# Expert layers of a macaron block: routing in one piece with gathered tiles, or by batches with rows scattered to regions

## The reference, cut to what matters

```python
x = x + 0.5 * ffn(layernorm(x), ...)
x = x + attn(layernorm(x), ...)          # 16 heads of 8, rotary, causal
x = x + 0.5 * ffn(layernorm(x), ...)

def ffn(x, Wr, br, ln_g, ln_b, W1, b1, W2, b2):   # 8 experts, one for each token
    p = softmax(xt @ Wr + br)
    gates, idx = max(p), argmax(p)
    xn = layernorm(xt) * ln_g + ln_b               # 128 features
    h = relu(xn @ W1[idx] + b1[idx])               # 512 wide
    y = (h @ W2[idx] + b2[idx]) * gates
```

## Time and profile before

| | us |
|---|---|
| median of three runs | 973.03 |
| the profiled execution | 971.15 |
| its span, first to last instruction | 969.2 |
| busy: TensorE / VectorE / ScalarE / GpSimd | 781.0 / 658.9 / 530.0 / 354.1 |
| first expert layer, until its last write-back is issued | 0 to 180 |
| attention with its projections | 188 to 793 |
| output projection | 794 to 810 |
| second expert layer | 810 to 969 |

### The profile page before, as it was taken

One profiled execution on the slowest core, in us unless ns is written; L12 is line 12 of the kernel. 1 busy time (PEld: TensorE's weight loads), 2 busy tenths in 40 slices (PEclk: granted clock), 3 DMA queues, 4 the chain that ended last, 5 costly groups with the idle time before them and its releaser, 6 DMA issues. The chain is left out here.

```text
span 969.2 us, 17210 instructions
## 1 busy us (share of the span) xinstructions
PE 781.0 (81%) x5494; PEld 426.3 (44%) x5494; DVE 658.9 (68%) x1821; ACT 530.0 (55%) x1126; POOL 354.1 (37%) x635
## 2 busy tenths in 40 slices
PE   2839777258459999999999999999999988578874
PEld 2838777234212333333333333333333337567773
DVE  4475565279867787787877878778787209656563
ACT  1206666215404667766677666766667643146663
POOL 5006777217812222332223322233222210047774
PEclk9659999769856999999999999999999779589998
DMA  9062222214572022210222102221020000532221
GB/s 323 34 174 71 76 74 72 64 36 116 155 189 35 2 50 52 50 44 10 50 51 51 43 10 50 51 50 43 10 51 3 1 1 1 146 81 73 78 77 24
DMA packets 42083, 62.32 MB, mean 64 GB/s; under 512 B 7843, under 2 KB 33453, under 8 KB 40592
## 3 DMA queue, kind: packets, MB, share of 16 engines
q1 hardware_dynamic: 33248, 45.76, 18.7%
q0 software_dynamic: 6240, 14.48, 5.6%
q10 hardware_dynamic: 2512, 1.06, 0.4%
HBM read 39.87 MB, written 21.92 MB: 64 GB/s over the span
## 5 line engine op out<-in xcount | busy, mean ns | idle before, releaser
L1235 DVE CUSTOM_DVE_ANT_0 cst<-psS,cst 128x768 bf16<-128x768 f32 (+7 forms) x512 | 364.4, 755 | 103.0 <-PE psS L1109 100.7
L1199 ACT ACTIVATE prob<-psST 128x512 f32<-128x512 f32 (+3 forms) x768 | 323.8, 495 | 143.3 <-PE psST L1134 139.8
L1148 PE MATMUL a_psO<-prob,vs 128*32 128x512 f32 (+3 forms) x1536 | 168.5, 511 | 0.9 <-POOL prob L1320 0.7
L1319 POOL TENSOR_TENSOR a_gate<-a_zeros 1x1 f32<-1x1 f32 x128 | 23.6, 184 | 335.1 <-ACT prob L1199 335.1
L1134 PE MATMUL psST<-a_qs,ks 75*128 75x512 bf16 (+1 forms) x480 | 123.9, 327 | 5.7 <-ACT prob L1199 3.3
L654 POOL DMA_INDIRECT g_row<-rows,f_there_number x78 | 77.8, 998 | 133.3 <-SPq L500 110.1
L1109 PE MATMUL psS<-ks,a_qs 72*128 72x512 bf16 (+2 forms) x480 | 116.6, 332 | 5.3 <-DVE a_rowmax L1235 5.2
L1109 PE MATMUL psS<-ks,qs 72*128 72x512 bf16 (+3 forms) x288 | 76.6, 359 | 24.5 <-DMA qs<-q_split 17.1
L555 PE MATMUL g_psH<-g_xnT,g_w1s 128*128 128x128 f32 x624 | 83.6, 277 | 2.4 <-ACT g_xnT L583 2.4
L1134 PE MATMUL psST<-qs,ks 75*128 75x512 bf16 (+3 forms) x288 | 80.3, 351 | 6.3 <-ACT prob L1199 5.1
L565 PE MATMUL g_psY<-g_w2s,g_hidT 128*128 128x128 f32 x624 | 83.4, 277 | 1.1 <-ACT g_hidT L590 1.1
(11 more groups left out here) (154 smaller groups left out, 923.0 us busy)
## 6 DMA issues: line engine op xcount, KB each, us to landing
ks<-k_split SPq DMA_DIRECT2D x48, 192.0 KB
rows<-tok SPq DMA_DIRECT2D x8, 1028.0 KB, 11.1
a_qs<-q_split SPq DMA_DIRECT2D x60, 96.0 KB
k_split<-p_part SPq DMA_DIRECT2D x40, 128.0 KB, 2.3
qs<-q_split SPq DMA_DIRECT2D x36, 96.0 KB
q_split<-p_part SPq DMA_DIRECT2D x24, 128.0 KB, 2.3
w<-in_Wb SPq DMA_DIRECT2D x1, 2064.0 KB, 10.7
w<-in_W SPq DMA_DIRECT2D x1, 2048.0 KB, 15.8
```

Source lines behind the costliest of these rows:

```text
L1148: last = nc.tensor.matmul(psO[32 * h:32 * h + 32, c0:c0 + w], vs[r][:, j, h, :], prob[:, u % RING, h, 0:w], start=(j == 0), stop=(u + 1 in ...
L1199: nc.scalar.activation(prob[:, u % RING, h, 0:w], psST[(u * QH + h) % 3][:, 0:w], ACT.Exp, scale=SCALE).then_inc(exp_done, 1)
L1235: last = nc.vector.tensor_tensor_reduce(out=out[:, a * CH:a * CH + width], in0=ps[:, a * CH:a * CH + width], in1=mask_row[:, S - width:], ...
```

## The change

The output projection moves into the second layer's block. Routing goes by four batches of 1024 tokens (TB = 8 columns). TensorE's order is a list: project (second layer), router, ranks. VectorE does `statistics(b)` and `choose(b)`; the reciprocal roots are made without ScalarE, by a shifted integer as a first value and three Newton steps, for both norms at once. ScalarE normalises four of a batch's eight columns, VectorE the others. A token's place is known once its batch is ranked: each expert has its own region of 4224 rows in DRAM, `base` carries on how far each is filled, and GpSimd scatters the batch's eight columns there by 128 rows of 1032 bytes (the token's number is now the last column). The slot and tile matrices, their 64 products, the store of `tok` and the gathers go. `tables` computes each tile's expert and first row. SP writes 128 rows of padding behind each region, waits for the scatters, and loads the tiles as blocks of consecutive rows, up to eight ahead; GpSimd keeps the write-back alone, its indices read from the row itself. Everything of a layer is one block. The weights are loaded only after x has arrived, and the warm-up before the tile loop is 28 x 4 products, queued behind `ranks(3)`. Not shown below: `choose` is the selection of before on 64 columns a batch; ScalarE follows TensorE's list (normalisations and copies for a router, copies for a project, the exponential for ranks); the tile loop's code for TensorE, ScalarE and VectorE is as before; `tables` is 17 small steps.

```diff
-TW = 2 * D + 1
-HALF_GATE = 2 * D
+TW = 2 * D + 2
+HALF_GATE, TOKEN = 2 * D, 2 * D + 1
...
-WARM = (18, 16)
+WARM = (18, 28)
+SCATTERS, YR = 4, 4
...
+REGION = B * S + P
+PADS = E * REGION
...
 def load_weights(sp, n):
 
+    for b in range(B):
+        sp.wait_ge(n.x_loaded[b], 16)
...
+        order = []
+        if r == 1:
+            order += [("project", 0), ("project", 1)]
+        order += [("router", 0), ("router", 1)]
+        for b in range(B):
+            if r == 1 and b + 2 < B:
+                order.append(("project", b + 2))
+            order.append(("ranks", b))
+            if b + 2 < B:
+                order.append(("router", b + 2))
...
+            def statistics(b):
+                sl = slice(b * TB, (b + 1) * TB)
+                if r == 0:
+                    dve.wait_ge(n.x_loaded[b], 16)
+                for g in range(b * PB, (b + 1) * PB):
+                    if r == 1:
+                        dve.wait_ge(projected, g + 1)
+                        x = n.tok[:, g * CB:(g + 1) * CB, 0:D]
+                        nc.vector.tensor_tensor(x, x, out_ps[g % 2][:, :].rearrange("p (j d) -> p j d", j=CB),
+                                                ALU.add).then_inc(added, 1)
+                        dve.wait_ge(added, g + 1)
+                    for t in range(g * CB, (g + 1) * CB):
+                        link.then(nc.vector.bn_stats(n.stats[:, t, :], n.tok[:, t, 0:D]))
+                link.join()
+                mean, var = n.mean[:, sl], n.var[:, sl]
+                even, odd, sq_even, sq_odd = (n.stats[:, sl, k] for k in (1, 4, 2, 5))
+                link(nc.vector.tensor_tensor(mean, even, odd, ALU.add))
+                link(nc.vector.tensor_scalar(mean, mean, 0.5, None, ALU.mult))
+                link(nc.vector.tensor_tensor(var, sq_even, sq_odd, ALU.add))
+                link(nc.vector.tensor_tensor(even, even, odd, ALU.subtract))
+                link(nc.vector.scalar_tensor_tensor(even, even, 0.25, even, ALU.mult, ALU.mult))
+                link(nc.vector.scalar_tensor_tensor(var, var, 1.0 / D, even, ALU.mult, ALU.add))
+                sh, ro, co = shift[:, b, :, :], root[:, b, :, :], corr[:, b, :, :]
+                link(nc.vector.tensor_scalar(shift[:, b, 0, :], var, EPS, None, ALU.add))
+                link(nc.vector.tensor_scalar(shift[:, b, 1, :], var, 1.0 + EPS, EPS * EPS, ALU.mult, ALU.add))
+                link(nc.vector.tensor_scalar(ro.bitcast(I32), sh.bitcast(I32), 1, None, ALU.logical_shift_right))
+                link(nc.vector.tensor_scalar(ro.bitcast(I32), ro.bitcast(I32), -1.0, FIRST_ROOT, ALU.mult, ALU.add))
+                for _ in range(3):
+                    link(nc.vector.scalar_tensor_tensor(co, ro, -0.5, ro, ALU.mult, ALU.mult))
+                    link(nc.vector.tensor_tensor(co, co, sh, ALU.mult))
+                    link(nc.vector.scalar_tensor_tensor(ro, co, 1.5, ro, ALU.add, ALU.mult))
+                nc.vector.scalar_tensor_tensor(offset[:, sl], mean, -1.0, root[:, b, 1, :],
+                                               ALU.mult, ALU.mult).then_inc(scales_ready, 1)
+                for t in range(b * TB + 1, (b + 1) * TB, 2):
                     nc.vector.tensor_scalar(n.shared[:, t, :], n.tok[:, t, 0:D], n.mean[:, t:t + 1],
+                                            root[:, b, 1, t % TB:t % TB + 1],
+                                            ALU.subtract, ALU.mult).then_inc(odd_normed, 1)
+                link(nc.vector.tensor_tensor(inv_u[:, sl], shift[:, b, 1, :], root[:, b, 1, :], ALU.mult))
+                link(nc.vector.tensor_tensor(inv_u[:, sl], inv_u[:, sl], root[:, b, 0, :], ALU.mult))
...
+                dve.wait_ge(ranks_done, b + 1)
+                link(nc.vector.tensor_tensor(rk, part(b, 1), base[:, b, :].unsqueeze(1).to_broadcast([P, TB, E]),
+                                             ALU.add))
+                dve.wait_ge(onehot_ready, b + 1)
+                link(nc.vector.tensor_tensor(rk, rk, onehot[:, sl, :], ALU.mult))
+                link(nc.vector.reduce_sum(pk, rk, AX.X))
+                nc.vector.tensor_copy(place[:, sl], pk).then_inc(placed, 1)
+                link(nc.vector.tensor_tensor(base[:, b + 1, :], base[:, b, :], part(b, 2)[:, 0, :], ALU.add))
...
+            statistics(0)
+            statistics(1)
+            choose(0)
+            for b in range(2, B):
+                statistics(b)
+                choose(b - 1)
+            choose(B - 1)
+            tables()
+            dve.wait_ge(tiles_known, 2)
...
+            def project(g, u):
+                pe.wait_ge(turned_copied, u + 1)
+                wait(pe, added, g - 1)
+                for j in range(CB):
+                    last = nc.tensor.matmul(out_ps[g % 2][:, j * P:(j + 1) * P], xT[u % 2][:, j * P:(j + 1) * P],
+                                            n.wproj[:, 5, :], start=True, stop=True)
+                last.then_inc(multiplied, 1)
+                pe.wait_ge(multiplied, u + 1)
+                pe.sem_inc(projected, 1)
...
+            warm_up(nc, pe, n, psW, WARM[1])
...
+            rows = n.rows_dram[r]
+            sp.wait_ge(pool_chain, 2)
+            sp.dma_start(rows[PADS:PADS + P, :], pad[:, :]).then_inc(pads_stored, 16)
+            sp.wait_ge(counted, 1)
+            for e in range(E):
+                at = sp.value_load(pad_row[0:1, e:e + 1], min_val=e * REGION, max_val=e * REGION + B * S)
+                sp.dma_start(rows[ds(at, P), :], pad[:, :]).then_inc(pads_stored, 16)
+            sp.wait_ge(pads_stored, 16 * (E + 1))
+            for k in range(SCATTERS):
+                sp.wait_ge(scattered[k], 16 * NT // SCATTERS)
+            sp.wait_ge(tiles_known, 2)
+            for t in range(NS):
+                k = t % LR
+                at = sp.value_load(tile_row[0:1, t:t + 1], min_val=0, max_val=PADS)
+                wait(sp, y_stored[t % YR], 16 * ((t - LR) // YR + 1))
+                sp.dma_start(row[k][:, :], rows[ds(at, P), :]).then_inc(loaded[k], 16)
...
+            sent = 0
+            for b in range(B):
+                pool.wait_ge(gates_ready, b + 1)
+                pool.wait_ge(placed, b + 1)
+                for t in range(b * TB, (b + 1) * TB):
+                    wait(pool, scattered[sent % SCATTERS], 16 * (sent // SCATTERS))
+                    pool.indirect_dma_start(
+                        out=n.rows_dram[r][:, :],
+                        out_offset=bass.IndirectOffsetOnAxis(ap=place[:, t:t + 1], axis=0),
+                        in_=n.tok[:, t, :], in_offset=None).then_inc(scattered[sent % SCATTERS], 16)
+                    sent += 1
```

More of the change, by code:

```diff
@@ L271, in ffn @@
 def ffn(nc, n, r, target):
[L277 to L279 removed]
+    G = NT // CB
+    PB = TB // CB
+    with ExitStack() as ctx:
         def sb(name, shape, dt=F32):
[L281 to L370 removed]
@@ L417, in _ @@
[L417 to L427 removed]
+                link(nc.vector.tensor_tensor(last[:, :], first[:, :], ntile[:, :], ALU.add))
```

685 lines of the change are left out of this document (299 added, 386 removed).

## The result

The changed kernel takes **980.35 us** in the median of 20 runs (971.72 to 983.23), the kernel before 966.58 (20 runs, 962.56 to 975.91): a ratio of 1.0119, 95% interval 1.0095 to 1.0144. The forecast was 970 with most of its weight on faster or no change; it is slower, by 1.2%. The forecast also started from a median of three runs, 973.03, that lies 6.45 above the median of twenty. The profiled execution of the changed kernel took 981.57 us, its span is 979.6. To see what belongs to the change I also use a second pair of traces, from another chip: spans of 964.3 before and 970.4 after.

What follows compares the result with a forecast made beforehand. GpSimd's write-back and gather issues were taken to bound the tile loop. -39.3 + 4.8 + (1.1 to 5.9) + (23.4 to 33.0) = -10.0 to +4.4, taken -2.8: 968.4, about 970 us against the median; range 952 to 992.

Steps and rivals of the forecast that it cites:

- the middle: Whole kernel: the value taken within the sum's -10.0 to +4.4 us, -2.8, from routing clocks of 0.56 and 0.84.
- 38 steps, two layers: Tile loop without gathers: 2.03 us a step, 77.1 a layer in place of 97.2 and 96.3, so -39.3 us.
- first transpose, layer one: Layer one's routing in four batches: first transpose at 76.7 to 81.5 us instead of 75.61, +1.1 to +5.9.
- first projection addition to first transpose, layer two: Layer two's routing with projection: first transpose at 881.0 to 890.6 us instead of 857.59, +23.4 to +33.0.
- restart at half clock: Tile loop's start: warm-up ends 12 us early, first tiles run at 1.2 GHz, 2.4 us lost a layer, +4.8.
- the cold end: Routing with TensorE at the low clock throughout: the upper ends of its terms, +4.4 us for the whole sum.
- twenty small steps at 0.205: Routing, VectorE's statistics of each batch: mean, variance, shift trick and Newton rounds take 4.1 us.
- four of eight normalisations at 0.26: Routing, VectorE's statistics of each batch: its share of the normalisations takes 1.0 us, the other four go to ScalarE.
- The attention is not touched: Attention, 203 to 793 us, most of the span: left out of the forecast's sum as unchanged.
- the rival of slow scatters: Routing: GpSimd's scatters slower than its gathers; at 2.0 us each, 11 us a layer, 992 in all; chance 0.13.
- a loop near 2.6: Tile loop: SP's load or a row buffer's return comes late, step stays near 2.6 us, about 1009; chance 0.07.
- everything at its good end: Routing keeps 2.4 GHz (10.0 us gained), tiles run at 1.92 (8.4 more): about 955; chance 0.32.

Runs made afterwards that it cites:

- e_weights: The changed kernel with the weights loaded only after the first batch's gates are known: 991.69 us, 0.963 of the kernel before on its chip.
- e_dummy: The changed kernel with four kinds of VectorE operations run once on scratch ahead of layer one's first batch: 996.19 us, 0.964 of the kernel before.
- a_att: The changed kernel with unused TensorE products filling two idle stretches at the attention's start: 992.24 us, 0.963 of the kernel before on its chip.
- b_att: The kernel before with unused TensorE products filling two idle stretches at the attention's start: 1041.66 us, 1.006 of the unedited kernel before on its chip.
- e_poolloads: The changed kernel with block loads issued by GpSimd, one behind every write-back, in place of SP: 1038.19 us (one run).
- e_hoist: The changed kernel with VectorE's read of the expert number put ahead of the weigh addition: 977.01 us, 0.945 of the kernel before on its chip.
- e_twice3: The changed kernel with the last batch's eight scatters sent twice in each layer: 1003.28 us (one run).
- e_order: The changed kernel with layer two's projections one place earlier in TensorE's and ScalarE's order: 983.16 us, 0.954 of a kernel before of 1032.5.

## Why the prediction was wrong

From the profile of before (span 969.2) to that of after (979.6), beside the middle that I took:

| term | forecast | measured |
|---|---|---|
| 38 steps, two layers | -39.3 | -16.5 and -15.1 = -31.6 |
| first transpose, layer one | +1.1 to +5.9, taken +3.5 | 87.51 - 75.61 = +11.9 |
| first projection addition to first transpose, layer two | +23.4 to +33.0, taken +28.2 | 91.6 - 59.9 = +31.7 |
| restart at half clock | +4.8 | from transpose to first bias addition, 3.2 for 2.07, twice = +2.3; the rest is in the steps |
| attention | 0 | -2.6 |
| all else | 0 | -1.3 |
| sum | -10.0 to +4.4, taken -2.8 | +10.4 |

The two sums are 13.2 us apart. Layer one's first transpose makes 8.4 of it, 2.4 by the middle and 6.0 beyond even the cold end; the steps and the restart make 5.2; layer two's first transpose makes 3.5, all of it by the middle; the attention and all else take 3.9 off. So more than one step failed: the middle cost 5.9, and with the cold end, +4.4, the sum would still have been 6 us short.

**The first step that failed is "so I take the middle, -2.8".** I had put the sum's cold end at +4.4 and argued for a mixture from 0.56 and 0.84 of before's clock. The same section said that routing is now spread thinner. The traces show 0.50 from 20 to 64 us and 0.50 to 0.57 over most of layer two's routing, and waits at, and 0.3 to 0.7 us beyond, the upper ends. The Trainium skill, TensorE: Matmul & The Clock Gate, "HAM oscillation — how this bites in real kernels", which stood beside it as my upper end, was the better guide. What spoke for the middle was the 0.84, and that was one execution's number: in the second trace of before the same stretch of 13.9 us, from 805.6 on, has 0.67.

**Two terms were mis-sized.** The step is 2.12 and 2.14, not 2.03: 3.5 and 4.1 us, of which the first two steps, at half clock (2.84 and 3.13, 2.84 and 3.26), make 1.9 and 2.0. 1.995 and 1.92 were read from tiles whose rows lay ready, with the register read already in them; at full load it falls on the path more often. And "twenty small steps at 0.205" with "four of eight normalisations at 0.26" holds for every batch but layer one's first, which has 7.1 us of stretched operations, more than the middle cost. This the trace of before does show, in a row that I had not taken up: an operation that takes 0.18 us when it comes again took 2.74 (3.50 in the second trace). VectorE, profile of before:

```profile
20.89 2.74 DVE L256 TENSOR_SCALAR f_small<-var 128x32 f32<-128x32 f32 x1
```

By e_weights the weights' transfers are not the cause, by e_dummy most of it is not the first use of a kind.

**One term was not there at all.** "The attention is not touched" was taken to mean that it lasts the same. It does not: 590.4 to 600.6 us, by where TensorE's clock comes back at its start and whether it falls once more near its end. In the profiles it even helped (-2.6), since before's fell in a long case too. How it weighs in the medians stays open. Nine of 13 runs of before on the second chip lie within 2.2 us of the fastest, only two of ten of the changed kernel lie near its 972, and this goes with TensorE's clock: the two have a mean granted clock of 0.885, the five from 981 on 0.872 to 0.874 (before: 0.908 to 0.913 in the nine, 0.894 to 0.905 in the four slower ones). But outside the attention the spans of the first pair differ by 13.0 us and those of the second by 6.9, the difference being in layer two, whose clock has phases too. The medians are 12 to 14 apart. So four traces do not say how much of this is the attention's phase and how much layer two's, and a_att and b_att did not settle it.

**What held.** The loop was bound by GpSimd's two issues (0.30 us between them, row after row), and a load left on GpSimd costs about 0.4 us a step (e_poolloads); VectorE's register read is the next bound (e_hoist); scatters issue at 1.27 for a forecast of 1.3 and their queue of sixteen is the path (e_twice3), so the rival of slow scatters is out, as is that of a loop near 2.6 by the steps of 2.12 and 2.14; the 0.96 us next to VectorE's routing (the scatter at 53.96, for one, beside the normalisations of 53.94 to 55.05) is also no more than the gather's, so the Trainium skill's lock-out of GpSimd (SBUF — State Buffer, "Who interferes with whom") changes nothing that this trace shows. Layer two's waits are the projections ahead of the ranks (e_order). The rival "everything at its good end" needed 2.4 GHz in routing, which no run kept.

## What to carry to other kernels

Where a forecast has a cold and a warm end of the clock, decide by what the change does to TensorE's gaps, not by halving: here the work cut into thinner pieces got the cold end. A clock share read from one trace may be that execution's alone. Price the first pass through new code apart from the later ones. Before a stage is said to be untouched, compare its length in several executions. And in a queue that issues both results and loads, an issue can cost more than its time, where the load stands behind a wait.

## What the runs showed of the hardware

Chips differ, and not by a factor. The kernel before takes 967 to 968 us on three and 1033 on two. On one of these two a trace was taken of its loop (b_att), and there the loop with two GpSimd transfers a tile has a step of 3.29 us for 2.54 and a wait about every 14 us, while the changed kernel's step, where its loop is as it was, is 2.08 to 2.16 on all. There the changed kernel with edits that gained nothing (e_weights, e_dummy) is 3.6 to 3.7% faster than the kernel before, so the sign of this change depends on the chip. Its routing is slower on these two: in layer one the waits for the ranks of choices 1 and 2 are 3.6 to 4.7 us for 2.8 and 2.9, and the pad writes are slow; SP's timeline of e_order, where the profile after has 8.49:

```profile
72.22 19.88 SPq L708 DMA_DIRECT2D rows<-f_pad  x8
94.36 1.92 SPq L717 DMA_DIRECT2D f_row<-rows  x2
```

Eight register reads and issues took 19.88 us, ended 5.3 us after the last scatter was issued (86.8) and set the first load, at 94.36 instead of 85.35. What slows both on these two chips, the runs don't say. Nor do they say what stretches the same operations of the first batch to 3.47 and 0.73 us in every trace of the changed kernel that I read there.
